# Two uneven batches of norms, their unit vectors spread over turns, and two fills moved to the last turns

## The reference

```
y    = affine(conv1x1(x, fc1))                       # 48 -> 48 channels
win  = 8x8 windows of y; 64 nodes of 48 channels each
xn   = nodes / max(norm(nodes), 1e-12)               # unit vectors
dist = |xn|^2 - 2 xn.xn + |xn|^2;  idx = the 9 nearest nodes of each node
h    = max over the 9 of gelu(edge_affine([x_i, x_j - x_i]))
x1   = affine(conv1x1(h, fc2)) + x
then: a ConvLSTM over the 32 rows of x1, forward and backward,
      projection, batch norm, relu, + x1
```

## Time and profile before

| | |
|---|---|
| median of three executions | 727.64 us |
| profiled execution, its own time | 725.73 us |
| its span in the trace | 723.9 us |
| mean granted TensorE clock | 0.927 of full speed |
| busy in the span | PE 629.2, DVE 511.7, ACT 547.9, POOL 106.9 us |
| head (to the first gather) | 0 to 75.15 us |
| 32 turns, and the last results | 75.15 to 384.84 us |
| scan and output | 384.84 to 723.9 us |

### The profile page before, as it was taken

The page is one execution under the profiler, slowest core; times in us unless marked ns, Lnnn a source line. Parts: engine busy times, 40 slices in busy tenths (PEclk is TensorE's granted clock), DMA queues, the critical chain, the costliest instruction groups (busy, mean ns, idle before and its releaser), DMA issues.

```text
span 723.9 us, 16291 instructions
## 1 busy us (share of the span) xinstructions
PE 629.2 (87%) x4532; PEld 462.9 (64%) x4532; DVE 511.7 (71%) x1169; ACT 547.9 (76%) x1059; POOL 106.9 (15%) x98
## 2 busy tenths in 40 slices
PE   7785763999999999999857999999999999999930
PEld 1123532555555555555527999999999998888910
DVE  2678670899999999989984666666666666666635
ACT  4631460788888888888864999999999888888845
POOL 2400310232222222233232000000000000300000
PEclk9975685999999999999987999999999999999965
DMA  8856698556656565566420000000001221176216
GB/s 214 274 160 176 162 110 110 123 129 126 132 130 137 133 138 131 124 125 132 103 56 20 23 22 22 22 22 22 22 22 45 64 64 48 56 151 141 72 54 174
DMA packets 102889, 72.22 MB, mean 100 GB/s; under 512 B 54798, under 2 KB 90128, under 8 KB 102144
## 3 DMA queue, kind: packets, MB, share of 16 engines
q1 hardware_dynamic: 102864, 71.92, 43.7%
HBM read 47.37 MB, written 22.35 MB: 96 GB/s over the span
## 4 chain that ended last, share of the span: by engine, by line
PE 70%; DMA 7%; ACT 7%; issue 6%; DVE 5%; SPq 2%; POOL 1%; DVEq 0%; ACTq 0%
PE pz L674 39%; PE pz L589 14%; PE p_out L597 4%; DMA y_hl<-y_d 4%; ACT gel L767 3%; PE p_keys L537 3%; PE p_edge L550 2%; PE p_edge L685 2%; ACT selfg L761 2%; PE p_edge L552 2%; DMA x_in<-xs 1%; PE pz L509 1%; DVE hmax L1076 1%; DVE y_sb L1239 1%; ACT ab_lo L753 1%
## 5 line engine op out<-in xcount | busy, mean ns | idle before, releaser
L1076 DVE TENSOR_REDUCE hmax<-gel 96x128 f32<-96x1024 f32 x128 | 154.3, 1206 | 46.0 <-ACT gel L767 45.3
L767 ACT ACTIVATE gel<-pz 96x1024 f32<-96x1024 f32 x128 | 130.8, 1023 | 71.7 <-PE pz L589 68.0
L674 PE MATMUL pz<-xh_hi,wl_hi 112*112 (+1 forms) x768 | 140.1, 291 | 5.5 <-POOL xh_lo L974 5.5
L674 PE MATMUL pz<-xh_hi,wl_lo 112*112 (+1 forms) x768 | 135.5, 285 | 0.0
L674 PE MATMUL pz<-xh_lo,wl_hi 112*112 (+1 forms) x768 | 135.3, 285 | 0.0
L674 PEld LDWEIGHTS pz<-xh_hi,wl_hi 112*112 112x112 f32 x768 | 107.8, 176 | 22.0 <-issue 9.4
L674 PEld LDWEIGHTS pz<-xh_hi,wl_lo 112*112 112x112 f32 x768 | 107.9, 177 | 0.0
L674 PEld LDWEIGHTS pz<-xh_lo,wl_hi 112*112 112x112 f32 x768 | 107.8, 177 | 0.0
L1176 DVE SCALAR_TENSOR_TENSOR h<-to,tc 48x256 f32<-48x256 f32 x128 | 53.7, 419 | 35.4 <-ACT tc L853 33.5
L1182 DVE TENSOR_TENSOR xh_lo<-h,xh_hi 48x256 f32 (+1 forms) x124 | 48.3, 416 | 33.3 <-ACT xh_hi L864 33.3
L974 POOL TENSOR_TENSOR xh_lo<-kl,xh_hi 48x512 f32 (+1 forms) x32 | 38.0, 1188 | 187.2 <-DVE idx L1052 96.7
(11 more groups left out here) (115 smaller groups left out, 930.5 us busy)
## 6 DMA issues: line engine op xcount, KB each, us to landing
ib<-idx_d SPq DMA_DIRECT2D x64, 256.0 KB, 4.3
y_d<-y SPq DMA_DIRECT2D x32, 192.0 KB, 3.4
y_hl<-y_d SPq DMA_DIRECT2D x32, 192.0 KB, 4.2
hist_d<-h SPq DMA_DIRECT2D x128, 48.0 KB, 1.6
hp<-hist_d SPq DMA_DIRECT2D x32, 192.0 KB, 2.6
kr<-xn_d SPq DMA_DIRECT2D x32, 98.0 KB
xn_d<-x_in SPq DMA_DIRECT2D x32, 96.0 KB, 2.2
kl<-xn_d SPq DMA_DIRECT2D x32, 96.0 KB
```

The costliest lines, as they stand in the source:

```text
L674: mm = pe.matmul(o, wgt[0:TOP, d, m, t], rhs, start=(n == 0), stop=(n == 8))
L767: act.activation(gel[:, t % 2], pz[0:O, 2 * (t % 2):2 * (t % 2) + 2, :], ACT.Gelu) \
L1076: dve.tensor_reduce(dst, gel[:, t % 2].rearrange("p w (r c k) -> p w r c k", r=WS, k=KN), AX_X, ALU.max).then_inc(S["maxed"], 1)
```

## The change

1. The norms come in batches of 4 and 12 chunks (`FIRST`, `REST`). `inverses(0)` stands after chunk 4 on DVE where it stood after chunk 9, and `inverses(1)` behind the first one-hot matrices. `keys` of groups 0 and 1 stand inside PE's loop over chunks.
2. The 12 chunks of the second batch are made into unit vectors inside turns 0 to 11: chunk 4+t is spread by PE in turn t (`inverse`, between `gather(t,3)` and `keys(t+4)`), multiplied by DVE at the end of its turn t, and stored by SP at the start of its turn t+1. Turns 0 to 11 are unrolled for it (`SPREAD` = 6 pairs). `inverse` writes `p_out`, the PSUM bank that `own` and `fc2` use, so that `own(g)` waits until the multiply of turn g-2 is done.
3. `fill_rows` moves from SP's turn 1 to its turn 27 (`GROUPS - 5`), and `pads` from before POOL's turn 0 to the start of its turn 26.

```diff
+FIRST = 4
+REST = CHUNKS - FIRST
+SPREAD = REST // 2
         def p_inv(c):
-            if c < CHUNKS // 2:
+            if c < FIRST:
                 return p_keys[:, :] if c % 2 else pz[:, 3]
-            return pz[:, c % 4]
+            return p_out[:, :]
...
         def turns(engine, turn):
-            for b in range(2):
-                turn(0, b)
-            with engine.Fori(1, GROUPS // 2 - 3) as j:
+            for j in range(SPREAD):
+                for b in range(2):
+                    turn(j, b)
+            with engine.Fori(SPREAD, GROUPS // 2 - 3) as j:
...
             def store_xn(c):
                 sp.wait_ge(S["xn_done"], c + 1)
+                if c >= FIRST:
+                    sp.wait_ge(S["xn_stored3"], 32 * (c - FIRST + 1))
...
             def turn(j, b):
-                if isinstance(j, int) and nth(j, b, 0)[0] == 1:
+                if isinstance(j, int) and 0 < 2 * j + b < 2 * SPREAD:
+                    store_xn(FIRST + 2 * j + b - 1)
+                if isinstance(j, int) and j == SPREAD - 1 and b == 1:
+                    store_xn(CHUNKS - 1)
+                    sp.wait_ge(S["xn_stored3"], 32 * (REST + 1))
+                if isinstance(j, int) and nth(j, b, 0)[0] == GROUPS - 5:
                     fill_rows()
...
             def own(g, b, n):
...
+                if not isinstance(g, int) or g >= 2:
+                    pe.wait_ge(S["xn_done"], min(FIRST + g - 1, CHUNKS) if isinstance(g, int) else CHUNKS)
+                elif g == 0:
+                    pe.wait_ge(S["nrm_ready"], 2)
...
                 gather(g, 3, b)
+                if isinstance(j, int) and 2 * j + b < REST:
+                    inverse(FIRST + 2 * j + b)
                 on(4, keys)
...
             def turn(j, b):
+                if isinstance(j, int) and nth(j, b, 0)[0] == GROUPS - 6:
+                    pads()
...
-            pads()
             turns(pool, turn)
...
                 self_max(*now)
+                if isinstance(j, int) and 2 * j + b < REST:
+                    normed(FIRST + 2 * j + b)
```

More of the change, by code:

```diff
@@ L345, in store_x1 @@
                         .then_inc(S[f"x1_stored{b}"], 16)
-            for c in range(3):
+            for c in range(6):
                 store_y(c)
+            store_unit(0)
             sp.wait_ge(S["pads_set"], 4)
-            sp.wait_ge(S["y_stored0"], 32)
+            sp.wait_ge(S["y_stored0"], 64)
             load_y(0, 0, 0)
             load_y(1, 1, 0)
[L353 to L356, removed]
+            store_y(6)
+            store_y(7)
             store_xn(0)
             store_xn(1)
-            store_y(11)
+            store_y(8)
             store_xn(2)
+            store_xn(3)
+            store_y(9)
+            store_y(10)
             sp.wait_ge(S["xn_stored0"], 64)
@@ L497, in norms @@
             def norms(c):
-                q, at = c // (CHUNKS // 2), c % (CHUNKS // 2)
+                q, at, of = batch(c)
                 pe.wait_ge(S["y_sq_ready"], c + 1)
-                pe.matmul(p_nrm[q][0:CHUNKS, :], sel_sb[:, c, CHUNKS * q:CHUNKS * q + CHUNKS], y_sq[:, c % 3],
-                          start=(at == 0), stop=(at == CHUNKS // 2 - 1)).then_inc(S["nrm_done"], 1)
+                rows = slice(2 * FIRST * q, 2 * (FIRST * q + of))
+                pe.matmul(p_nrm[q][0:2 * of, :], sel_sb[:, c, rows], y_sq[:, c % 3],
+                          start=(at == 0), stop=(at == of - 1)).then_inc(S["nrm_done"], 1)
             def chunk(c):
@@ L521, in inverse @@
                     pe.wait_ge(S["xn_done"], c - 1)
[L522 to L525, removed]
+                if q == 1:
+                    pe.wait_ge(S["z2_ready"], at)
+                pe.matmul(p_inv(c), pick[0:32 + 2 * REST, 2 * at:2 * at + 2].rearrange("p h n -> p (h n)"),
+                          inv_hl[0:32 + 2 * REST], start=True, stop=True).then_inc(S["inv_mm"], 1)
             def keys(g, b, n):
@@ L626, in _ @@
                     edges_rest(0, 0, 0)
+                    pe.wait_ge(S["xn_done"], FIRST)
+                    keys(0, 0, 0)
                 if c == 14:
                     edges(1, 1, 0)
-                if 11 <= c < 15:
-                    inverse(2 * c - 22)
-                    inverse(2 * c - 21)
+                    keys(1, 1, 0)
             norms(CHUNKS - 1)
[L633 to L637, removed]
+            own(0, 0, 0)
             keys(2, 0, 1)
-            for c in range(12, CHUNKS):
-                inverse(c)
-            own(0, 0, 0)
             keys(3, 1, 1)
-            pe.wait_ge(S["xn_done"], CHUNKS)
             turns(pe, turn)
@@ L739, in roots @@
                     act.wait_ge(S["unit_ready"], 1)
-                act.activation(nrm[:], p_nrm[q][0:CHUNKS, :], ACT.Sqrt).then_inc(S["nrm_ready"], 1)
+                rows = 2 * (REST if q else FIRST)
+                act.activation(nrm[0:rows], p_nrm[q][0:rows, :], ACT.Sqrt).then_inc(S["nrm_ready"], 1)
             def ab_high(g, b, n):
@@ L912, in _ @@
                 rows = slice(32 * s, 32 * s + 32)
-                pool.tensor_copy(pick[rows], own[rows, rows.start:rows.start + CHUNKS, 0:1]
-                                 .to_broadcast([32, CHUNKS, HALF])).then_inc(S["pick_set"], 1)
+                pool.tensor_copy(pick[rows], own[rows, rows.start:rows.start + 2 * REST, 0:1]
+                                 .to_broadcast([32, 2 * REST, HALF])).then_inc(S["pick_set"], 1)
                 pool.wait_ge(S["pick_set"], s + 1)
@@ L1117, in turn @@
                         scan_weights(part)
-            for c in range(10):
+            for c in range(FIRST + 1):
+                chunk(c)
+            inverses(0)
+            for c in range(FIRST + 1, 8):
                 chunk(c)
@@ L1126, in _ @@
                 .then_inc(S["t2_ready"], 1)
-            inverses(0)
-            for c in range(10, 14):
+            for c in (8, 9):
+                normed(2 * c - 16)
+                normed(2 * c - 15)
                 chunk(c)
-                normed(2 * c - 20)
-                normed(2 * c - 19)
-            chunk(14)
-            chunk(15)
+            for c in range(10, 13):
+                chunk(c)
             for part in range(2):
                 topk(0, 0, 0, part)
-            inverses(1)
+            chunk(13)
+            chunk(14)
             for part in range(2):
                 topk(1, 1, 0, part)
-            for c in range(8, 12):
-                normed(c)
+            chunk(15)
             dve.wait_ge(S["masks_set"], 7)
@@ L1143, in _ @@
                 one_hot(0, 0, 0, half)
-            for c in range(12, CHUNKS):
-                normed(c)
+            inverses(1)
             for part in range(2):
```

80 lines of the change are left out of this document (37 added, 43 removed).

## The result

The changed kernel takes 741.88 us (median of four executions, 740.22 to 745.04) where the kernel before took 726.42 in four (724.40 to 728.04): ratio 1.0209, 95% interval 1.0174 to 1.0245. It is slower, by 15 us; whether by 2% or more is left open by the interval. The forecast was 734: the sign was right, the size of the loss was twice what the sum gave (+7.4). The time lies near rival 3's 742, but not by its mechanism: from turn 1 to turn 11 the granted clock stays at 1.00. The profiled execution took 740.22 us with a span of 738.3, 14.4 longer than before.

The account below looks back on a forecast made before the run. PE was taken as bound by a y load behind the fills in turn 2, steady turns by a PE and ACT chain with DVE nearly full. -5.7 + 0 - 20.9 + 22.2 + 11.8 = +7.4; forecast 734, range 719 to 742.

Parts of the forecast that it names:

- rival 3: Spread turns: clock drops to 1.2 GHz in some, with pads and stall at their upper ends; 742 us; chance 12%.
- Late stall: Turn 28, ahead of `edges`: PE stands 19.2 us for a y load behind the moved fills, then slow clock; +22.2 us.
- Rival 1: Turn 28: the late fills land before PE needs the y load, so 22.2 us fall away; 712.8 us; chance 13%.
- The estimate by the Trainium skill: Fills reach four of 16 ports, a quarter of 435 GB/s: 20 us for 2.17 MB, turn 28's stall 14 us.
- Early stall: Turn 2: PE's wait for the y load behind the fills, and its cold clock, go; -20.9 us.
- Spread chunks: Turns 1 to 12: PE's added matmul and `own` waiting for DVE's multiply, turn 9.68 instead of 8.60; +11.8 us.
- Rival 2: Spread turns: only PE's matmul costs, DVE's multiply fills idle time; 4 us instead of 11.8, 727 us; chance 20%.
- only the wait, +0.74: Turn 12, last of the spread turns: no added matmul, only `own` waiting for DVE's multiply; +0.74 us.
- Head: Before turn 0: earlier reciprocals bring the first gather to about 69.6 instead of 75.2; -5.7 us.
- The bound I had named for the head (-2): Before turn 0: if key loads and index DMAs take two us longer each, the change is -2 us.
- Pads: Turn 0 gains 2.0 us without memsets beside one-hot operations, turn 26 loses the same 2.0; 0 in sum.

Follow-up runs that it names:

- Experiment 1: Kernel before with only the fills moved to SP's turn 27 and the pads to POOL's turn 26; 722.17 us, ratio 0.9920.
- experiment 3: Changed kernel with DVE's multiply of a spread chunk between maxima 2 and 3 instead of behind `self_max`; 727.83 us, ratio 0.9996 to the kernel before.
- experiment 2: Changed kernel with chunk 15's store in SP's turn 12 and the wait for all stores in turn 13; 740.52 us, ratio 1.0190 to the kernel before.
- experiment 8: The changed kernel run again, nothing altered; 742.91 us, ratio 1.0223 to the kernel before.
- Experiment 9: Changed kernel with key loads of groups 0 and 1 ahead of the y stores of chunks 9 and 10; 738.52 us, ratio 1.0165 to the kernel before.
- experiment 7: Changed kernel with multiply between maxima 2 and 3, chunk 15's store in turn 12, fills in 16 pieces ahead of `spread_idx`; 701.40 us, ratio 0.9672 to before.

## Why the prediction was wrong, step by step

- **Late stall** (+22.2, measured +20.9): right in place, cause and size. The idle time was 19.0 for 19.2. Experiment 1 shows the exchange by itself. Rival 1, that the fills hide, is out: 84 GB/s and not 195. The estimate by the Trainium skill (SBUF — State Buffer, "Door 1: The DMA port swizzle") would have made this stall 14 us; the fills took as long late as early, 29.1 us to land, so the row was the better price.
- **Early stall** (-20.9): gone as said.
- **Spread chunks** (turn of 9.68, measured 9.89; +11.1 in turns 0 to 11, measured +13.9): the mechanism, `own` waiting for the multiply, is shown by the rows and by experiment 3. Its size was 0.2 us too small per turn: the multiply ended at 2.80 of the turn (2.70 in the sum), and `own` followed 0.14 behind it where I had let 0.06 pass. Turn 1, which I had taken as cold and with the matmul alone, has the wait too (1.12 us): without the pads it is no longer cold. Rival 2 (4 us) is out for this order of DVE's work; with the multiply moved it is nearly what happens (8.76).
- **The step that failed is turn 12 with "only the wait, +0.74"**. I took SP's added work as 0.9 us of issues and the stores as traffic, and asked of the last of the twelve only what PE and DVE do. I did not ask what SP waits for: in turn 11 the order on SP holds a store whose data are ready a turn later than those of the other ten, plus a wait for all stores to land. Both lines stand in the diff. That cost 5.5 us (experiment 2 gives them back in the place; in the time they show only as 1.4 and, on experiment 3, 3.0, both within the intervals). With the store moved, turns 12 and 13 take 18.1 us, 0.9 more than before, which is the +0.7 of the sum.
- **Head** (-5.7, measured -2.5, and -0.7 in experiment 8, the same kernel again): a second term that was mis-sized. By DVE's chunk 4 the sum had 46.1 us to the first gather and it took 50.6, so 4.5 is missing; that only 3.2 of it show is luck, since chunk 4 itself began 1.4 earlier than before. 0.4 is a slip in the sum: 59.6 + 10.3 is 69.9, not 69.6. From `keys(0)` to the first gather it took 22.5, as the terms rightly added say. The other 4.1 lie ahead of `keys(0)`. SP's first issue behind chunk 5 went out 0.8 late, the 24 issues took 14.2 us where I had 11.2 (0.93 for two), and the load took 0.35 more. The issues are the term that was mis-sized. They follow one another without a gap, most at the price I took, but several take 0.6 to 1.4 us each: the stores of unit vectors took 2.39 and 2.25 us for four and those of y of chunks 6 and 7 took 2.80, where I had 1.86 for four. Why some take longer is open. Experiment 9 takes four of the 24 from ahead of the load, which the sum too would have priced at 1.9 of its 2.6 us; even so `keys(0)` came 25.5 us after chunk 4 (49.04 - 23.55) where the sum had 24.0 with all 24. The bound I had named for the head (-2) held in this profile and not in that of experiment 8.
- **Pads** (0; measured about -3.5): moving them away from turns 0 and 1 gave 4.1 us in experiment 1 and not 2.0, since before PE's turn 1 also began at a clock of 0.50 and took 1.9 us longer for it, a term that the sum leaves out. In turn 26 two one-hot operations beside memsets took 0.83 and 1.02 us and not 2.70, see below, and the turn lost 0.6 (a pitch of `fc2` of 9.18 where its neighbours have 8.5 to 8.6) and not 2.0. This miss is the other half of the luck in turns 0 to 11. The timeline of POOL and DVE there:

```profile
321.70 0.83 DVE L1071 TENSOR_SCALAR onehot<-ib,jcol_sb 128x1024 fp32r<-128x1024 uint16 x1
323.42 1.15 POOL L964 MEMSET xh_lo<- 64x544 f32 x1
324.10 1.02 DVE L1071 TENSOR_SCALAR onehot<-ib,jcol_sb 128x1024 fp32r<-128x1024 uint16 x1
```

Both misses are SP's, but not of one kind: at the seam an issue waited for data, which I had not asked about; in the head the issues waited for nothing and took longer than the one pair of rows that I had priced them by.

## What to carry to other kernels

A stall from one large transfer does not go away by being moved; cut into pieces that go out where the queue's engine waits anyway, it does (20 us here, while the same pieces at another place in the same turn gave back more than half). When an operation joins a full engine, ask who waits for its end and put it ahead of work that nobody waits for: one place in DVE's order was worth 14 us. And of every issue moved in a hand-written queue, write down when its data are ready, first and last turn apart, beside what the issue costs.

## What the runs showed of the hardware that I had not expected

- SP issued two DMAs of 1060 KB in 0.71 and 0.63 us, and then stood 22.9 us at the next issue, of a small load (23.0 to 23.9 in the seven other profiles that have the fills in one piece). Sixteen times two pieces of 66 KB held up nothing, at a DMA share of 0.95 in the window of experiment 7.
- The one-hot operation of DVE takes 0.74 us alone, 2.70 beside a memset of POOL in turn 0 before, and 0.83 and 1.02 beside memsets of the same shape in turn 26. What makes the difference was not tried.
- In the head of the changed kernel SP's 28 issues between 31.57 and 48.13, one behind the other and none held by missing data, took between 0.32 and 1.36 us each; what a longer one meets isn't shown.
- The same head differs from one execution to the next: DVE's chunk 4, which in most profiles waits for the first store of y, began between 22.08 and 24.95 us in kernels whose order up to there is the same. This is as large as some of the effects looked for, and a single profile can't tell a change of 2 us in the head unless it is measured from that point on.
